# Graph layer with GNN, linear attention and expert FFN: 127-partition loads in two pieces, sample tables earlier, one more staged chunk in the sort stage, FFN block gathers moved into the GNN loop

## The chip, the core and the metric

One core of one Trainium2 chip runs the kernel. The metric is the device time of one execution in microseconds. Times inside the run are those of one profiled execution. The engines are called TensorE (PE in rows; PEld is its weight load), VectorE (DVE), ScalarE (ACT), GpSimd (POOL) and SyncE (SP); a row with SPq, ACTq or POOLq is the issue of a DMA by that engine.

## What is computed

There are 6250 nodes with 256 features, x. The reference, cut to what matters:

```python
xn = layernorm(x)
x = x + gnn(xn, src, dst) + mix(xn)        # gnn: 100000 edges sorted by dst
x = x + ffn(layernorm(x))                  # ffn: 131072 edges, not sorted
# gnn, per head: e = leaky(e_src[src] + e_dst[dst])
#   out[n] = sum over edges with dst = n of softmax(e) * z[src]
# mix: linear attention; k = softmax over nodes, context = k^T v, q softmax over dims
# ffn: graph attention gives scores per expert; top 2 of 4 experts, GELU FFN each
```

Edges of one graph lie sorted by dst, 784 (GNN) or 1024 (FFN) on each of 128 partitions, 100000 = 127 * 784 + 432. The softmax and sum over the edges of a node is then a scan along each partition.

## The kernel before

The program is a row of blocks, each a list of instructions per engine that runs in order; an all-engine barrier ends each block. Order inside an engine is the order written; between engines there are semaphores only. Three blocks are touched.

**Sort and projection** (`project`, L645). VectorE sorts the FFN edges by dst with a bitonic network (`dve_stages`); between pieces of it, `sort_on(n)`, it makes layernorm statistics of x (`stats`, `norm`, in 7 groups of 7 tiles). TensorE turns and projects each tile into rows z (L816), ScalarE copies them out, SyncE stores them in HBM (`gnn_rows`). Then TensorE makes keys and values (L410), and ScalarE stores v rows in HBM.

In the same block the place where each node's edges begin is found (`search_parts`, L241): dst comes in (L714: 127 partitions; the tail of 432 on partition 127 through GpSimd, L764), VectorE copies it to `edges` and takes every 28th as `few` (L926 to L929, `dst_ready`). SyncE writes `few` and `edges` to HBM (L717, L718) and reads `few` back twice, the second time one row lower, `table[0:127]` into `above[1:128]` (L272 to L274). VectorE compares all nodes with row starts (`dve_first`, L281) and splits the differences of samples (`dve_rise`, L287 to L300); TensorE multiplies both (`pe_samples`, L309); VectorE counts and gives a block number per node (`dve_blocks`, L315 to L325). GpSimd then gathers one block of 28 dst per node, 50 indirect DMAs (`pool_blocks`, L331), VectorE counts in it (`dve_base`, `dve_places`, L337 to L367), and GpSimd scatters row starts (`scatter_starts`, L965, 50 DMAs). Before them GpSimd has issued the loads of Wqkv (L766) and src (L768, L770), with x's groups coming through ScalarE's queue (0 and 1) and SyncE's (2 before `dst_ready`, 3 to 6 after the samples).

When z is stored, GpSimd gathers z rows by src, one indirect DMA per column of 128 edges. The GNN loop later goes over 56 chunks of 14 columns with 4 buffers (`got`). Six chunks, `STAGED`, don't go straight into a buffer: GpSimd gathers them ahead in halves of 7 columns into `staged` (`pool_half`, L450), SyncE writes each half to HBM (`sp_half`, L457), and in the loop one large load brings a chunk back (`sp_staged`, L1417). `STAGED_WITH_SORT` of the six are done in this block, and behind them the first two chunks are gathered into their buffers (`first_gathers`, L1215).

**Keys** (`key_context`, L1072). GpSimd gathers the other staged halves, then chunks 2 and 3. VectorE takes the maximum of k over nodes (L1172), subtracts it (L1190), and does the search for the FFN graph as above up to block numbers (L277 to L325), then spreads row starts over edges (`dve_all`, L1013 to L1054) and scales the context (L1200). ScalarE takes exp. TensorE sums k^T v (L1146) over 13 loads of v with two buffers; after the sixth load's sums stand the sample products of the search (L309), and at the end two small turns for `dve_all`. SyncE's list: search samples, row starts, v loads 0 and 1, three staged halves, then alternately one v load and one of the remaining halves. A v load from the third on waits for the sums two loads before.

**GNN loop** (`gnn_edges`, L1583). Per chunk c VectorE makes logits (L1296 to L1317), weighs the gathered rows (L1367) and scans (L1391); ScalarE takes exp, weighs one head (L1378), writes states out (L1407); TensorE and the others do one tile of the attention output beside. GpSimd gathers chunk c from 4 on into buffer c modulo 4 (`pool_gather`, L1277, 14 DMAs) once chunk c - 4 is weighed, unless c is staged. After the loop it gathers the 50 blocks of the FFN search (`pool_blocks`, L331). SyncE stores states and tiles and ends by waiting for them. The next block (`carry`) begins with a barrier and uses the gathered blocks.

Of the kernel before, what the change touches and what calls it, by code (L numbers as in the profile page):

```python
# [16 lines left out]
P = 128  # L17
# [9 lines left out]
NS = NT + 1  # L27

# [9 lines left out]
STAGED = (8, 14, 21, 28, 36, 44)  # L38
STAGED_WITH_SORT = 4
# [80 lines left out]
class Kernel:  # L120
# [120 lines left out]
    def search_parts(self, g, stack):  # L241
# [22 lines left out]
        class Steps:  # L264
# [5 lines left out]
            def sp_samples(sp):  # L270
# [3 lines left out]
                sp.dma_start(above[1:P, :], table[0:P - 1, :]).then_inc(samples_in, 16)  # L274
# [9 lines left out]
            def dve_rise(dve):  # L284

                dve.wait_ge(samples_in, 32)
# [358 lines left out]
    def project(self, kv, kv_done, parts, later, staging):  # L645
# [7 lines left out]
        with ExitStack() as here:  # L653
# [25 lines left out]
                     "dst_tail_in", "src_tail_in", "wqkv_in",  # L679
                     "stats_made", "root_made", "norm_ready", "xn_ready", "turned", "xt_ready", "projected", "z_evac", "xt_out", "starts_out", "minus_set")  # L680
            (padded, dst_in, dst_ready, samples_out, blocks_out, w_in, att_clear, w_turned, w_ready, zeroed, seg_clear, src_in,
             dst_tail_in, src_tail_in, wqkv_in,
# [28 lines left out]
            def _(sp):  # L711
                sort.sp_load(sp)
                sp.wait_ge(padded, 1)
                sp.dma_start(dst_i[0:full, :], io["dst"][0:full * GNN.width].rearrange("(p w) -> p w", w=GNN.width)).then_inc(dst_in, 16)  # L714
                load_x(sp, 2)
# [5 lines left out]
                for g in range(3, LOADS):  # L721
                    load_x(sp, g)
# [30 lines left out]
                sp.wait_ge(src_tail_in, 16)  # L753
                sp.wait_ge(wqkv_in, 16)
# [5 lines left out]
            def _(pool):  # L760
# [4 lines left out]
                               io["dst"][full * GNN.width:GNN.edges].rearrange("(p w) -> p w", p=1)).then_inc(dst_tail_in, 16)  # L765
                pool.dma_start(self.wqkv[:, :, :], io["L0_mix_Wqkv"].rearrange("(k p) c -> p k c", p=P)).then_inc(wqkv_in, 16)  # L766
# [3 lines left out]
                pool.dma_start(self.edge_src["gnn"][0:full, 0:GNN.width],  # L770
                               io["src"][0:full * GNN.width].rearrange("(p w) -> p w", w=GNN.width)).then_inc(src_in, 16)
# [8 lines left out]
                pool.wait_ge(src_tail_in, 16)  # L780
                for j in range(2 * STAGED_WITH_SORT):
                    staging.pool_half(pool, j)
# [110 lines left out]
            def _(dve):  # L893
# [30 lines left out]
                dve.wait_ge(dst_in, 16)  # L924
# [5 lines left out]
                dve.drain()  # L930
                stats(0)
# [3 lines left out]
                find.dve_first(dve, later)  # L935
                find.dve_rise(dve)
# [135 lines left out]
    def key_context(self, kv, kv_done, stack, find, context, later, parts, staging):  # L1072
# [6 lines left out]
        with ExitStack() as mine:  # L1079
# [23 lines left out]
            def _(sp):  # L1103
# [12 lines left out]
                halves = iter(range(2 * STAGED_WITH_SORT, 2 * len(STAGED)))  # L1116
                for j in (next(halves), next(halves), next(halves)):
                    staging.sp_half(sp, j)
                for g in range(SLOTS, loads):
                    load_v(g)  # L1120
                    for j in halves:
                        staging.sp_half(sp, j)
                        break
# [459 lines left out]
    def gnn_edges(self, fin, finm, parts, ctx, find):  # L1583
# [7 lines left out]
        with ExitStack() as here:  # L1591
# [41 lines left out]
            def _(pool):  # L1633
                def step(c, b, u, i):
# [1091 lines left out]
```

## Time and profile before

| | us |
|---|---|
| median of 3 runs | 2831.59 (2829.88 to 2832.51) |
| the profiled execution | 2831.12 |
| its span, first to last instruction | 2829.3 |
| sort and projection | 0 to 336.9 |
| keys | 336.9 to 438.9 |
| GNN loop | 438.9 to 1354.5 |
| all that follows | 1354.5 to 2829.3 |

The span is what the trace covers, 1.8 us less than the execution's time. Busy over the span: VectorE 74%, GpSimd 69%, TensorE 53%, ScalarE 46%. These shares are means over stages with different limits, so a stage has to be read by itself: by who comes last to its barrier, and what that engine waited for. An idle time in brackets behind an instruction is the time its engine stood before it, and the arrow names what ended it; "issue" is time in which it waited for nothing that the profile shows.

### The profile page before, as it was taken

How to read it: one execution, taken by the hardware profiler on the slowest of the kernel's cores; microseconds unless marked ns; L12 is line 12 of the kernel's file. 1: busy time of each engine (PE TensorE's matmuls, PEld its weight loads, DVE VectorE, ACT ScalarE, POOL GpSimd, SP SyncE). 2: the span in 40 equal slices, each digit the busy share in tenths (PEclk: the TensorE clock that was granted, in tenths of full speed). 3: DMA queues.
4: the chain of work that ended last, by engine and by line, in shares of the span. 5: the costliest groups of instructions: out<-in, count | busy, mean ns of one | idle time of the engine just before them, and what ended most of it. 6: DMA issues, size and time to landing. Idle time of an engine off the chain costs nothing. (4 is left out here: it accounts for less than half of the span.)

```text
span 2829.3 us, 22764 instructions
## 1 busy us (share of the span) xinstructions
PE 1511.8 (53%) x5476; PEld 938.2 (33%) x5476; DVE 2083.0 (74%) x3305; ACT 1302.0 (46%) x3173; POOL 1943.4 (69%) x1982
## 2 busy tenths in 40 slices
PE   2766440123232323331152399999999999984223
PEld 2533140011111111110052266555555555551023
DVE  6988769899999999995493566556555555567557
ACT  2622116799999999995152122222222222220022
POOL 1677675767777777777466877777777777777560
PEclk9978775555555555555555699999999999997666
DMA  5717664777777877774651322222222222222195
GB/s 160 238 28 207 200 207 143 261 243 257 252 252 259 274 237 274 242 244 140 190 163 48 100 51 51 54 53 62 52 53 51 51 50 51 50 57 40 34 317 220
DMA packets 225713, 418.38 MB, mean 148 GB/s; under 512 B 51232, under 2 KB 174733, under 8 KB 218156
## 3 DMA queue, kind: packets, MB, share of 16 engines
q1 hardware_dynamic: 133504, 278.19, 27.8%
q0 software_dynamic: 75920, 123.77, 19.6%
q10 hardware_dynamic: 16156, 14.98, 1.6%
q8 instruction: 44, 0.72, 0.1%
q14 instruction: 89, 0.73, 0.1%
HBM read 216.03 MB, written 200.77 MB: 147 GB/s over the span
## 5 line engine op out<-in xcount | busy, mean ns | idle before, releaser
L1277 POOL DMA_INDIRECT stage_got<-ffn_rows,setup_src_ffn x860 | 839.3, 976 | 261.9 <-issue 261.8
L1277 POOL DMA_INDIRECT edges_got<-gnn_rows,edges_src_gnn x644 | 610.0, 947 | 246.7 <-issue 192.2
L1391 DVE TENSOR_TENSOR_SCAN stage_y<-stage_decays,stage_y 128x960 f32<-128x960 f32 (+2 forms) x256 | 520.7, 2088 | 5.8 <-issue 5.7
L2221 PE MATMUL stage_ph<-ffn_xt_all,stage_w 128*128 128x448 f32 x896 | 372.5, 555 | 98.7 <-ACT stage_start_parts L2282 39.6
L1407 ACT ACTIVATE stage_rows<-stage_y 128x3640 f32<-128x3640 f32 (+1 forms) x88 | 400.7, 4553 | 0.0
L2343 DVE TENSOR_TENSOR stage_start_parts<-stage_pk,stage_of_tile 128x490 f32<-128x490 f32 x328 | 209.4, 666 | 115.2 <-PE stage_pk L2213 110.9
L2213 PE MATMUL stage_pk<-stage_start_parts 128*128 128x490 bf16 x984 | 252.4, 396 | 65.5 <-DVE stage_start_parts L2343 51.0
L1693 PE MATMUL stage_pm<-setup_ident,stage_mix_parts 128*128 128x128 f32 x98 | 32.4, 434 | 432.6 <-ACT stage_mix_parts L1716 423.3
L1367 DVE TENSOR_TENSOR stage_y<-edges_got,stage_weights 128x896 f32<-128x896 f32 x168 | 262.6, 1665 | 0.3 <-ACT stage_weights L1346 0.3
L2221 PEld LDWEIGHTS stage_ph<-ffn_xt_all,stage_w 128*128 128x128 f32 x896 | 170.0, 192 | 236.5 <-issue 137.9
L2346 DVE TENSOR_REDUCE stage_got<-stage_start_parts 128x20 f32<-128x980 f32 x164 | 192.6, 1174 | 15.6 <-issue 0.9
L1349 ACT ACTIVATE stage_y<-stage_chunk_parts 128x128 f32<-128x128 f32 x32 | 9.9, 311 | 416.5 <-DVE stage_chunk_parts L1317 416.5
L2361 DVE TENSOR_TENSOR search_found<-stage_po,stage_b 128x512 f32<-128x512 f32 x112 | 70.0, 625 | 178.1 <-PE stage_po L2233 171.7
L1378 ACT ACTIVATE stage_y<-edges_got,stage_y 128x64 f32<-128x64 f32 x784 | 197.4, 422 | 0.0
L2233 PE MATMUL stage_po<-stage_w,stage_hid 128*128 128x256 f32 x784 | 183.9, 380 | 0.0
L2233 PE MATMUL stage_po<-stage_w,stage_start_parts 128*128 128x256 f32 x784 | 183.0, 380 | 0.0
L1693 PEld LDWEIGHTS stage_pm<-setup_ident,stage_mix_parts 128*128 128x128 f32 x98 | 14.2, 203 | 466.5 <-DVE stage_mix_parts L1766 453.4
L2213 PEld LDWEIGHTS stage_pk<-stage_start_parts 128*128 128x128 bf16 x984 | 93.8, 102 | 216.3 <-DVE stage_start_parts L2343 94.2
L2233 PEld LDWEIGHTS stage_po<-stage_w,stage_hid 128*128 128x128 f32 x784 | 150.7, 192 | 39.1 <-issue 18.2
L2233 PEld LDWEIGHTS stage_po<-stage_w,stage_start_parts 128*128 128x128 f32 x784 | 149.3, 190 | 36.5 <-issue 14.8
L1681 PE MATMUL stage_pq<-stage_mix_parts 128*128 128x256 f32 x196 | 100.1, 665 | 84.2 <-ACT stage_mix_parts L1730 84.2
L2282 ACT ACTIVATE stage_start_parts<-stage_ph,stage_b 128x896 f32<-128x896 f32 x56 | 55.1, 1007 | 192.1 <-PE stage_ph L2221 192.0
(483 smaller groups left out, 3099.5 us busy)
## 6 DMA issues: line engine op xcount, KB each, us to landing
state_gnn<-stage_rows SPq DMA_DIRECT2D x56, 1848.0 KB, 7.4
y<-search_found SPq DMA_DIRECT2D x28, 896.0 KB, 4.2
tail_fin_y<-y SPq DMA_DIRECT2D x7, 3584.0 KB, 17.1
stage_got<-ffn_rows,setup_src_ffn POOLq DMA_INDIRECT x860
state_ffn<-stage_rows SPq DMA_DIRECT2D x32, 384.0 KB, 2.4
edges_got<-gnn_rows,edges_src_gnn POOLq DMA_INDIRECT x700, 3.8
staged_rows<-rows_staged SPq DMA_DIRECT2D x12, 910.0 KB, 4.7
edges_got<-staged_rows SPq DMA_DIRECT2D x6, 1820.0 KB, 13.9
```

The lines of the kernel that those rows point to most:

```text
L1277: pool.indirect_dma_start(out=got[:, u, t, :], out_offset=None, in_=self.row_dram[g.name][:, :], in_offset=bass.IndirectOffsetOnAxis(ap=sr ...
L1367: ins = dve.tensor_tensor(of_head(h, s)[:, :, :, 0:n].rearrange("p q k t -> p t q k"), mine.rearrange("p t (q k) -> p t q k", q=Q), weight ...
L1378: ins = act.activation(of_head(h, s)[:, :, :, t], got[:, u, t, h * K:(h + 1) * K].rearrange("p (q k) -> p q k", q=Q), ACT.Copy, scale=y[:, ...
L1391: ins = dve.tensor_tensor_scan(some, r[s][:, 0:b - a, :].rearrange("p c t -> p (c t)"), some, 0.0, ALU.mult, ALU.add)
L1407: act.activation(rows[:, s, :, 0:C + H], y[:, s, :, 1:T + 1].rearrange("p c t -> p t c"), ACT.Copy).then_inc(rows_ready, 1)
L1681: mm = pe.matmul(pq[:, 0:D], xt[:, slot, k * P:(k + 1) * P], wq[:, k, :], start=(k == 0), stop=(k == 1))
L2213: mm = pe.matmul(pk[:, a, 0:(r1 - r0) * NT], chosen[:, c % 2, j * P:(j + 1) * P], table[:, n, r0:r1, :].rearrange("p r t -> p (r t)"), sta ...
L2221: mm = pe.matmul(ph[:, f % 2 * 2 + half, 0:HALF], w1[:, e, k, f * P:(f + 1) * P], xt_all[:, k, at(b * (B * P) + half * HALF, HALF)], start ...
L2233: mm = pe.matmul(po[:, bank, side:side + D], hid[s][:, f, t * P:(t + 1) * P], w2[:, e, f, :], start=(f == 0), stop=(f == FT - 1))
L2343: dve.tensor_tensor(masked[:, r0:r1, :], pk[:, a, 0:(r1 - r0) * NT].rearrange("p (r t) -> p r t", t=NT), of_tile[:, j, :].unsqueeze(1).to_ ...
L2346: dve.tensor_reduce(got[:, c % 2, T - picked(FFN, c) + j, :], masked, AX, ALU.add)
L2361: dve.tensor_tensor(yrow[:, k * 2:k * 2 + n, :], po[:, k % 2, 0:n * D].rearrange("p (t d) -> p t d", d=D), b2[:, e, :].unsqueeze(1).to_bro ...
```

## The change

Loads of 127 partitions are issued as 112 (`EVEN`) and 15: dst, src, and the read-back of the samples one row lower, in both searches. In the sort block, x's group 2 and Wqkv are issued after `dst_ready`, and `dve_first` and `dve_rise` come ahead of the statistics of group 0. Five staged chunks instead of four are gathered in the sort block; in the keys block SyncE writes the two halves left one after the other, ahead of the third v load. In the GNN loop GpSimd gathers 18 of the FFN blocks before chunk 4, five at each staged chunk, and two at the end.

```diff
+EVEN = P - 16
-STAGED_WITH_SORT = 4
+STAGED_WITH_SORT = 5
+BLOCKS_FIRST, BLOCKS_EACH = 18, 5
...
@@ sp_samples (L270), dve_rise (L284)
-                sp.dma_start(above[1:P, :], table[0:P - 1, :]).then_inc(samples_in, 16)
+                sp.dma_start(above[1:EVEN + 1, :], table[0:EVEN, :]).then_inc(samples_in, 16)
+                sp.dma_start(above[EVEN + 1:P, :], table[EVEN:P - 1, :]).then_inc(samples_in, 16)
...
-                dve.wait_ge(samples_in, 32)
+                dve.wait_ge(samples_in, 48)
...
@@ project, sync (L711)
-                sp.dma_start(dst_i[0:full, :], io["dst"][0:full * GNN.width].rearrange("(p w) -> p w", w=GNN.width)).then_inc(dst_in, 16)
-                load_x(sp, 2)
+                for a, b in ((0, EVEN), (EVEN, full)):
+                    sp.dma_start(dst_i[a:b, :], io["dst"][a * GNN.width:b * GNN.width].rearrange("(p w) -> p w", w=GNN.width)).then_inc(dst_in, 16)
...
-                for g in range(3, LOADS):
+                for g in range(2, LOADS):
                     load_x(sp, g)
...
@@ project, gpsimd (L760)
+                pool.wait_ge(dst_ready, 1)
                 pool.dma_start(self.wqkv[:, :, :], io["L0_mix_Wqkv"].rearrange("(k p) c -> p k c", p=P)).then_inc(wqkv_in, 16)
...
-                pool.dma_start(self.edge_src["gnn"][0:full, 0:GNN.width],
-                               io["src"][0:full * GNN.width].rearrange("(p w) -> p w", w=GNN.width)).then_inc(src_in, 16)
+                pool.dma_start(self.edge_src["gnn"][0:EVEN, 0:GNN.width],
+                               io["src"][0:EVEN * GNN.width].rearrange("(p w) -> p w", w=GNN.width)).then_inc(src_in, 16)
+                pool.dma_start(self.edge_src["gnn"][EVEN:full, 0:GNN.width],
+                               io["src"][EVEN * GNN.width:full * GNN.width].rearrange("(p w) -> p w", w=GNN.width)).then_inc(src_rest_in, 16)
...
@@ project, vector (L893)
-                dve.wait_ge(dst_in, 16)
+                dve.wait_ge(dst_in, 32)
...
+                find.dve_first(dve, later)
+                find.dve_rise(dve)
                 stats(0)
                 sort_on(1)
                 norm(0)
                 stats(1)
-                find.dve_first(dve, later)
-                find.dve_rise(dve)
                 norm(1)
...
@@ key_context, sync (L1103)
-                halves = iter(range(2 * STAGED_WITH_SORT, 2 * len(STAGED)))
-                for j in (next(halves), next(halves), next(halves)):
+                for j in range(2 * STAGED_WITH_SORT, 2 * len(STAGED)):
                     staging.sp_half(sp, j)
                 for g in range(SLOTS, loads):
                     load_v(g)
-                    for j in halves:
-                        staging.sp_half(sp, j)
-                        break
...
@@ gnn_edges, gpsimd (L1633)
+                few = self.search_few(FFN)
+
                 def step(c, b, u, i):
-                    if c >= GNN.slots and c not in STAGED:
+                    if c == GNN.slots:
+                        find.pool_blocks(pool, few, range(BLOCKS_FIRST))
+                    if c in STAGED:
+                        done = BLOCKS_FIRST + STAGED.index(c) * BLOCKS_EACH
+                        find.pool_blocks(pool, few, range(done, done + BLOCKS_EACH))
+                    elif c >= GNN.slots:
                         edge.pool_gather(pool, c, b, u)
                 in_quads(step)
-                find.pool_blocks(pool, self.search_few(FFN), range(NS))
+                find.pool_blocks(pool, few, range(BLOCKS_FIRST + len(STAGED) * BLOCKS_EACH, NS))
```

## Rows read from the trace of the kernel before

**Rows 1.** Busy time by stage: start:end, length, busy us (instructions) of each engine, TensorE clock, DMA share, GB/s.
```profile
0.00:336.90 336.90, 190.60 (x718) 109.71 (x718) 267.29 (x588) 111.59 (x336) 201.78 (x203) 0.85 0.53 160
336.90:438.90 102.00, 36.37 (x307) 33.62 (x307) 72.65 (x76) 13.12 (x8) 68.12 (x58) 0.68 0.62 194
438.90:1354.50 915.60, 236.56 (x496) 130.70 (x496) 847.63 (x987) 808.56 (x2116) 659.87 (x694) 0.50 0.71 238
```

**Rows 2.** VectorE in order of time, stage one: start, us, instruction [idle before <- what ended it].
```profile
35.21 0.57 DVE L926 CAST project_sorted_dst<-project_dst_i 128x784 f32<-128x784 int32 x1 [14.84 <-DMA project_dst_i<-in_dst_dram]
45.03 6.83 DVE L281 TENSOR_TENSOR edges_later_nodes<-setup_lane,project_search_gnn 128x6400 bf16<-128x6400 f32 x1
336.91 0.09 DVE L268 MEMSET earch_search_ffn_samples<- 1x32 f32 x1 [13.56 <-PEq L162]
```

**Rows 3.** Two stretches of stage one, columns as in the first group.
```profile
4.50:19.50 15.00, 0.00 (x0) 0.00 (x0) 8.57 (x34) 1.28 (x1) 2.97 (x5) 1.00 0.97 291
26.00:34.50 8.50, 2.25 (x12) 2.15 (x10) 0.00 (x0) 2.08 (x5) 0.00 (x0) 1.00 0.07 26
```

**Rows 4.** GpSimd in order of time, stage one.
```profile
61.42 1.08 POOL L331 DMA_INDIRECT search_found<-blocks_gnn,ject_search_gnn_at_block  x1 [53.94 <-DVE ject_search_gnn_at_block L325]
143.21 1.20 POOL L965 DMA_INDIRECT seg_gnn<-setup_start_rows_gnn,setup_seg_at_gnn  x1 [13.29 <-DVE setup_end_at_gnn L367]
327.90 0.95 POOL L1215 DMA_INDIRECT edges_got<-gnn_rows,edges_src_gnn  x1 [0.30 <-issue]
```

**Rows 5.** VectorE in order of time, stage two.
```profile
408.36 0.17 DVE L315 TENSOR_SCALAR search_search_ffn<-keys_tp 128x15 f32<-128x15 f32 x1 [23.50 <-PE keys_spread L309]
```

**Rows 6.** TensorE in order of time, stage two.
```profile
366.35 5.64 PE L1146 MATMUL keys_pkv<-keys_v_in,rows_X 128*128 128x129 f32 x32 [4.44 <-ACT rows_X L1162]
377.09 3.62 PE L1146 MATMUL keys_pkv<-keys_v_in,rows_X 128*128 128x129 f32 x16 [5.11 <-DMA keys_v_in<-v_rows]
394.58 5.20 PE L1146 MATMUL keys_pkv<-keys_v_in,rows_X 128*128 128x129 f32 x32 [13.87 <-DMA keys_v_in<-v_rows]
405.35 1.90 PE L309 MATMUL keys_tp<-ch_search_ffn_rise_parts,edges_later_nodes 128*128 128x33 bf16 x60
```

**Rows 7.** SyncE in order of time, stage two: issues, merged where alike.
```profile
370.21 0.37 SPq L1112 DMA_DIRECT2D keys_v_in<-v_rows  x1
387.30 0.32 SPq L457 DMA_DIRECT2D staged_rows<-rows_staged  x1
```

**Rows 8.** VectorE, the last chunk of the GNN loop.
```profile
1290.60 0.24 DVE L1296 TENSOR_TENSOR stage_chunk_parts<-edges_got,edges_ed_edge 128x56 f32<-128x56 f32 x1
```

**Rows 9.** Groups of GpSimd in stage three: count | busy us, mean ns | idle before, what ended it.
```profile
L1277 POOL DMA_INDIRECT edges_got<-gnn_rows,edges_src_gnn x644 | 610.0, 947 | 246.7 <-issue 192.2 <-DVE stage_y L1367 28.9 <-ACT stage_y L1378 25.6
L331 POOL DMA_INDIRECT search_found<-blocks_ffn,arch_search_ffn_at_block x50 | 49.8, 997 | 15.2 <-issue 15.2
```

**Rows 10.** GpSimd in order of time, first and last gather of stage three.
```profile
447.14 0.94 POOL L1277 DMA_INDIRECT edges_got<-gnn_rows,edges_src_gnn  x1 [24.05 <-ACT stage_y L1378]
1278.90 0.95 POOL L1277 DMA_INDIRECT edges_got<-gnn_rows,edges_src_gnn  x1 [0.30 <-issue]
```

**Rows 11.** Waits of SyncE around the end of stage three: us in total, times, longest.
```profile
SPq L1591 <- PEq L1591: 24.8, 1, 24.8
```

**Rows 12.** DMA issues: count, KB each, median us from issue to landing.
```profile
project_keys<-in_L_ffn_edge_index_dram SPq DMA_DIRECT2D x2, 512.0 KB, 5.5
samples_gnn<-project_few_dst SPq DMA_DIRECT2D x1, 14.0 KB, 2.4
keys_v_in<-v_rows SPq DMA_DIRECT2D x12, 516.0 KB, 5.7
edges_got<-gnn_rows,edges_src_gnn POOLq DMA_INDIRECT x700, 3.8
```

**Rows 13.** Groups of GpSimd, 130 to 336 us: the staged gathers of stage one.
```profile
L450 POOL DMA_INDIRECT rows_staged<-gnn_rows,edges_src_gnn x56 | 59.1, 1056 | 19.6 <-issue 16.5 <-DMA staged_rows<-rows_staged 1.7 <-DMA seg_gnn<-setup_start_rows_gnn,setup_seg_at_gnn 1.4
```

**Rows 14.** GpSimd, one staged gather of stage two.
```profile
367.53 1.63 POOL L450 DMA_INDIRECT rows_staged<-gnn_rows,edges_src_gnn  x1 [0.30 <-issue]
```

More of the change, by code:

```diff
@@ L678, in project @@
             names = ("padded", "dst_in", "dst_ready", "samples_out", "blocks_out", "w_in", "att_clear", "w_turned", "w_ready", "zeroed", "seg_clear", "src_in",
-                     "dst_tail_in", "src_tail_in", "wqkv_in",
+                     "dst_tail_in", "src_tail_in", "src_rest_in", "wqkv_in",
                      "stats_made", "root_made", "norm_ready", "xn_ready", "turned", "xt_ready", "projected", "z_evac", "xt_out", "starts_out", "minus_set")
             (padded, dst_in, dst_ready, samples_out, blocks_out, w_in, att_clear, w_turned, w_ready, zeroed, seg_clear, src_in,
-             dst_tail_in, src_tail_in, wqkv_in,
+             dst_tail_in, src_tail_in, src_rest_in, wqkv_in,
              stats_made, root_made, norm_ready, xn_ready, turned, xt_ready, projected, z_evac, xt_out, starts_out, minus_set) = (self.sem(here, n) for n in names)
@@ L753, in _ @@
                 sp.wait_ge(src_tail_in, 16)
+                sp.wait_ge(src_rest_in, 16)
                 sp.wait_ge(wqkv_in, 16)
@@ L780, in _ @@
                 pool.wait_ge(src_tail_in, 16)
+                pool.wait_ge(src_rest_in, 16)
                 for j in range(2 * STAGED_WITH_SORT):
```

## The prediction

> **What bounds the kernel now.** I read the span by stage first [rows 1]. The change touches the first three stages only (to 1354.5 us); the 1474.8 us behind them keep their code. A stage ends at a barrier, so in each one I ask which engine arrives last; the chain of waits covers only the end of the run and says nothing here.
>
> Stage one (sort and projection, to 336.9): VectorE stands 14.84 us before its copy of dst, and is done 13.56 us before the barrier opens [rows 2]. Meanwhile, the 26 to 34.5 us stretch has DMA at 0.07 of 16 engines and 26 GB/s [rows 3]: one engine carries the load's tail. The queue that is last is GpSimd's: its first block gather waits for VectorE until 61.42, its first scatter until 143.21, then it runs without pause to 328.9 (327.90 + 0.95), some 8 us ahead of the barrier [rows 4]. So GpSimd ends this stage, and VectorE moves GpSimd only through those two waits.
>
> Stage two (keys, to 438.9) ends with VectorE, which loses 23.50 us there, waiting for TensorE's sample products [rows 5]. TensorE has them behind six loads of v, and its longest pauses are for loads three and four [rows 6]. SyncE issues loads in the order written: after load three (370.21) it stands until 387.30 for a staged half that GpSimd has not gathered, and only then issues load four [rows 7].
>
> Stage three (GNN loop, to 1354.5): VectorE's last chunk starts at 1290.60 [rows 8]; after its last gather (1278.90) GpSimd issues 50 block gathers, 65.0 us, and the stage ends at 1354.5 [rows 9, 10]. SyncE, with all else stored, waits 24.8 us at this barrier [rows 11]. That overhang is what the third edit is aimed at.
>
> **The change, part by part.** The profiled execution took 2831.12 us, its span is 2829.3; the median of the three runs is 2831.59, 0.47 above. I sum against 2831.1.
>
> *dst as 112 + 15.* 388.9 KB at 26 GB/s is 15 us [rows 3], the length of the wait. What the split load takes isn't in this trace. Above: it lands no sooner (35.2). Below: one engine's 26 GB/s times 16 would be 1 us. The nearest row is the keys' 512 KB, 128 partitions on the same queue, 5.5 us from issue to landing [rows 12]; behind them, dst should land at about 13 to 16 us. VectorE needs it at 20.4 (35.21 less 14.84), so the whole wait of 14.84 goes; 5 us of slack stay.
> The Trainium skill's page "DMA: Bandwidth & Descriptors", section "Why a DMA increments its semaphore by 16 and not by 1", says a copy goes to the largest number of engines up to 16 that divides its outer dimension: 127 rows to 1, 112 to 16, 15 to 15. By that rule the load would be near the 1 us end, and the sum would be the same; the 0.07 share agrees with it for 127.
>
> *Samples first.* dst is ready at 21.3 instead of 36.1. The samples go out (2.4 us [rows 12]) and come back by three DMAs instead of two, one more issue of 0.3 us on SyncE: landed by about 27. VectorE covers this with its compare at L281, 6.83 us [rows 2], now ahead of stats(0), to 28.6. If the cover fails, the late side is a load like keys', 5.5 us, 2 us late: 0 taken, 2 kept for the range. x's third load and later ones are issued after the samples, and the 768 KB of Wqkv wait on GpSimd for dst; 5.4 MB at the 291 GB/s of the first busy stretch [rows 3] end at about 43 us; VectorE needs the third group, 1.7 MB with Wqkv beside it and so there at about 31, at 38, and the fourth past 50. GpSimd's src loads are behind Wqkv now and needed only by the staged gathers past 195: 0. Their split adds one issue on GpSimd, before the wait for VectorE: 0. Splitting the second search's samples adds one SyncE issue, before loads that nobody waits for yet: 0.
>
> *Stage one's end.* Both of GpSimd's waits come 15 us earlier. Then ten staged halves instead of eight: 14 more gathers at (59.1 + 19.6)/56 = 1.40 us [rows 13], 19.7 us. VectorE ends its sort 15 us earlier, and gathers that run after it cost 1.25 (rate of stage three, (610.0 + 192.2)/644 [rows 9]) instead of 1.35: some 18 of them, 2 us. GpSimd ends at 328.9 - 15 + 19.7 - 2 = 331.6. **Stage one: +2 us** (bounds -2 and +6); what VectorE gains is only waited longer at the barrier.
>
> *Stage two.* GpSimd has two staged halves left, done 18 us into the stage; SyncE stores both and then holds the v loads for TensorE's sums alone. In the old time base: loads one and two are summed from 366.35 on, 2.8 us each [rows 6]; load three is issued at 369.3 and lands, with the 5.7 us of its row [rows 12], at 375; three and four are summed to 381.2 (3.6 and 2.6 us), five issued at 378.6 and six at 381.2, six is summed by 389.5, and the samples take 3.0 (405.35 to 408.36): 392.5 against 408.36, 15.9 us earlier. With 6.9 us per load, as 370.21 to 377.09 shows, it is 13.5; with 4 it is 19. Behind the samples TensorE still has seven loads, as before, so the rest moves with it; 1 us off for pauses. **Stage two: -15 us** (bounds -20 and -9).
>
> *Stage three.* 48 of 50 block gathers go into the loop, ahead of GNN gathers: 18 first, five at each staged chunk. One is (49.8 + 15.2)/50 = 1.30 us [rows 9], the 48 are 62.4 us. GpSimd had idle time in the loop: 8.2 us at its start (438.9 to 447.14 [rows 10]), some 30 later, 8 at the end; less than 62. So GpSimd becomes the bound, and its queue is a floor: 644 gathers at 1.25 are 805, and 438.9 + 805 + 62.4 = 1306.3. The last rows land 2.9 later (3.8 from issue [rows 12], less 0.95): chunk 55 starts at 1309.2 instead of 1290.60, 18.6 us late. Bounds: 17.5 if the landing is quick, 24 with 1.40 per block gather. What follows chunk 55 is unchanged, and two block gathers lie beside it. The barrier opens 24.8 earlier for the overhang and 18.6 later for the loop. **Stage three: -6 us** (bounds -7 and 0).
>
> Sum: +2 - 15 - 6 = -19; 2831.1 - 19 = **2812 us**, 0.7% under the median.
>
> **The rivals.**
> 1. *The loop hides the block gathers.* VectorE was the loop's bound and GpSimd waited 28.9 + 25.6 us in it [rows 9]. Then chunk 55 keeps its time and stage three gives all 24.8: 2831.1 + 2 - 15 - 24.8 = 2793. Against: 24.05 of that idle is one wait, of which only 8.2 us lie in this stage. Chance 0.07.
> 2. *TensorE's wait is the v loads themselves.* If their latency, and not SyncE's order, sets loads four to six, stage two gives nothing: 2827. For: loads five to six also paused it. Against: the 17 us between two issues on SyncE. Chance 0.08.
> 3. *dst is no faster*, or the time goes to x and the keys' loads in front of it, so the split doesn't do what it says: GpSimd keeps its 61.42 and stage one is +17 instead of +2: 2827. Chance 0.06.
> 4. *Slower: VectorE holds up the inserted gathers.* In stage two, beside VectorE's large subtracts, a staged gather took 1.63 us instead of 0.95 [rows 14], 0.68 more. At that price 48 gathers add 33 us to a queue that is the bound: 2812 + 33 = 2845. It decides from 0.4 us each on (19/48). Against: the loop's gathers have a mean of 947 ns beside VectorE's scans and products [rows 9], no more than the quick ones anywhere. The Trainium skill's page "SBUF — State Buffer", section "Who interferes with whom", has VectorE and GpSimd share one port pair, which an instruction holds to its end. By that rule alone 2845 would be the time to expect wherever VectorE's instructions take the pair; the mean in the loop shows that they mostly don't there. Chance 0.06.
> 5. *Stages one and two give more* (quicker v loads, gathers at 1.25 throughout): 2803. Chance 0.08.
>
> **How the numbers follow.** The forecast has 0.65, with a range of its own from 2804 to 2821. Rivals 1 to 5 have 0.07, 0.08, 0.06, 0.06, 0.08. The range 2800 to 2828 takes in cases 2, 3 and 5 and leaves out 1 and 4 and some tails. A measurement tells 0.2% from no change here, 5.7 us: faster is below 2825.9. Rivals 2 and 3 fall within 0.2%, rival 4 is slower; faster 0.82, same 0.11, slower 0.07.
>
> **What would show it.** Stage one right: no wait of VectorE for dst, GpSimd's first block gather near 46, its last gather near 331, the stage's end near 339, with VectorE waiting over 25 us at the barrier. Stage two right: VectorE's 23.50 falls to 5 to 10, the loads of v follow each other without SyncE's gap, the stage takes 87 instead of 102. Stage three right: GpSimd without waits of any length, chunk 55's logits waiting for gathered rows, a loop 18 us longer and no overhang. It is wrong if GpSimd still waits for VectorE late in the loop (rival 1), if inserted gathers are longer than 1.1 us (rival 4), or if VectorE's dst wait stays (rival 3).

## The result, and the profile after

The changed kernel takes 2814.47 us (median of 4 runs, 2813.73 to 2815.70) against 2832.05 for the kernel before (4 runs on the same chip): a ratio of 0.9933, 95% interval 0.9919 to 0.9946, 17.6 us less. The profiled execution has a span of 2812.5 us, 16.8 under the 2829.3 of before. The windows by stage (start:end, length, busy us of PE, PEld, DVE, ACT, POOL, granted TensorE clock, DMA share, GB/s) answer to [rows 1]:

```profile
0.00:342.00 342.00, 192.25 (x718) 110.84 (x718) 267.45 (x588) 111.35 (x336) 217.28 (x217) 0.83 0.56 169
342.00:423.50 81.50, 33.19 (x306) 30.42 (x307) 72.71 (x76) 13.16 (x8) 54.62 (x44) 0.73 0.62 196
423.50:1334.40 910.90, 236.85 (x496) 130.69 (x496) 849.00 (x987) 807.15 (x2116) 660.52 (x695) 0.50 0.71 239
1334.40:2812.50 1478.10, 1046.33 (x3956) 663.36 (x3956) 896.98 (x1654) 368.25 (x714) 1017.30 (x1028) 0.84 0.34 86
```

| stage | before | after | difference | forecast |
|---|---|---|---|---|
| sort and projection | 336.9 | 342.0 | +5.1 | +2 |
| keys | 102.0 | 81.5 | -20.5 | -15 |
| GNN loop | 915.6 | 910.9 | -4.7 | -6 |
| the rest | 1474.8 | 1478.1 | +3.3 | 0 |
| span | 2829.3 | 2812.5 | -16.8 | -19 |

**Stage one.** VectorE in order of time (start, us, instruction, in brackets the idle time before it and what ended it), answering to [rows 2]:

```profile
19.99 0.57 DVE L934 CAST project_sorted_dst<-project_dst_i 128x784 f32<-128x784 int32 x1
...
21.78 6.83 DVE L284 TENSOR_TENSOR edges_later_nodes<-setup_lane,project_search_gnn 128x6400 bf16<-128x6400 f32 x1
31.27 0.19 DVE L290 TENSOR_TENSOR oject_search_gnn_samples<-oject_search_gnn_samples 128x28 f32<-128x28 f32 x1 [2.66 <-DMA oject_search_gnn_samples<-samples_gnn]
...
342.06 0.09 DVE L270 MEMSET earch_search_ffn_samples<- 1x32 f32 x1 [30.93 <-PEq L164]
```

The wait for dst is gone: the copy starts at 19.99 and nothing stands before it. In its place stands a wait of 2.66 us for the samples at L290, behind the compare that was to cover them. SyncE's issues show the samples on their way in time, and GpSimd's show what was issued beside them, and the waits that answer to [rows 4]:

```profile
23.51 1.11 SPq L276 DMA_DIRECT2D oject_search_gnn_samples<-samples_gnn  x1
24.67 0.44 SPq L277 DMA_DIRECT2D oject_search_gnn_samples<-samples_gnn  x1
```

```profile
21.20 0.79 POOL L771 DMA_DIRECT2D edges_got<-in_L_mix_Wqkv_dram  x1 [15.57 <-DVE project_few_dst L937]
...
49.26 1.07 POOL L334 DMA_INDIRECT search_found<-blocks_gnn,ject_search_gnn_at_block  x1 [25.69 <-DVE ject_search_gnn_at_block L328]
...
129.59 1.22 POOL L973 DMA_INDIRECT seg_gnn<-setup_start_rows_gnn,setup_seg_at_gnn  x1 [11.65 <-DVE setup_end_at_gnn L370]
...
331.91 0.95 POOL L1219 DMA_INDIRECT edges_got<-gnn_rows,edges_src_gnn  x1 [0.30 <-issue]
342.01 0.78 POOL L1011 IOTA keys_start_parts<- 128x784 int32 x1 [9.15 <-POOLq L164]
```

The samples' last read-back is issued at 24.67 and is there only at 31.27. In the microseconds ahead of it GpSimd issued Wqkv (768 KB, at 21.20) and src, and SyncE the 392 KB of block keys (at 21.32). In the five profiles with this order the wait is 1.41 to 2.66 us. GpSimd's first block gather moves from 61.42 to 49.26, 12.2 us where I had 15; from there to its last gather (331.91) it has one pause of length, the scatter's 11.65. What VectorE gained it waits for at the barrier, 30.93 us instead of 13.56.

**Stage two.** VectorE's 23.50 of [rows 5] is 2.89:

```profile
392.92 0.18 DVE L318 TENSOR_SCALAR search_search_ffn<-keys_tp 128x15 f32<-128x15 f32 x1 [2.89 <-PE keys_spread L312]
```

TensorE (where [rows 6] showed pauses of 5.11 and 13.87) and SyncE (where [rows 7] showed 17 us between two issues):

```profile
371.51 5.98 PE L1150 MATMUL keys_pkv<-keys_v_in,rows_X 128*128 128x129 f32 x32 [4.44 <-ACT rows_X L1166]
379.19 2.05 PE L1150 MATMUL keys_pkv<-keys_v_in,rows_X 128*128 128x129 f32 x16 [1.71 <-DMA keys_v_in<-v_rows]
...
385.10 2.05 PE L1150 MATMUL keys_pkv<-keys_v_in,rows_X 128*128 128x129 f32 x16 [1.38 <-DMA keys_v_in<-v_rows]
...
390.17 1.68 PE L312 MATMUL keys_tp<-ch_search_ffn_rise_parts,edges_later_nodes 128*128 128x33 bf16 x60 [0.65 <-DVE ch_search_ffn_rise_parts L303]
```

```profile
356.25 6.93 SPq L460 DMA_DIRECT2D staged_rows<-rows_staged  x2
375.37 0.37 SPq L1120 DMA_DIRECT2D keys_v_in<-v_rows  x1
```

SyncE issues the eleven later loads without a staged half between them. TensorE's pauses for the next four loads are 1.71, 0.42, 1.38 and 0.32 us, and the sample products start at 390.17 because VectorE's own operands (L303) come only then. The sums of one load take 2.05 us, where [rows 6] has 3.62 and half of 5.20. The windows of those sums, columns as in the windows by stage, first two of before, then one of after, differ in TensorE's granted clock: 0.55 and 0.73 of full speed, means of the two levels of 1.2 and 2.4 GHz, behind pauses of 5.11 and 13.87 us, against 1.00, the upper level throughout, behind one of 1.71:

```profile
377.05:380.75 3.70, 3.62 (x16) 3.43 (x16) 3.70 (x1) 0.76 (x1) 3.54 (x1) 0.55 0.14 37
394.58:399.80 5.22, 5.20 (x32) 5.01 (x32) 0.00 (x0) 0.00 (x0) 4.00 (x5) 0.73 0.80 232
379.19:389.55 10.36, 8.21 (x64) 7.44 (x64) 9.96 (x13) 3.40 (x2) 9.51 (x3) 1.00 0.68 209
```

From issue to landing a load of v takes 4.2 us, not the 5.7 of [rows 12] (count, KB each, median us):

```profile
keys_v_in<-v_rows SPq DMA_DIRECT2D x12, 516.0 KB, 4.2
```

Over the profiles with the new order it is 4.1 to 4.6 us; with the old order it is 5.7, and 4.9 in two others, so part of the 5.7 was that one profile's.

**Stage three.** GpSimd's groups (count, busy us, mean ns, idle before and what ended it) answer to [rows 9], then VectorE's logits, before and after:

```profile
L1281 POOL DMA_INDIRECT edges_got<-gnn_rows,edges_src_gnn x644 | 610.5, 948 | 196.2 <-issue 194.9 <-ACT stage_y L1382 0.9 <-DVE stage_y L1371 0.3
L334 POOL DMA_INDIRECT search_found<-blocks_ffn,arch_search_ffn_at_block x50 | 50.0, 1001 | 29.9 <-POOLq L164 14.9 <-issue 14.9
```

```profile
L1296 DVE TENSOR_TENSOR stage_chunk_parts<-edges_got,edges_ed_edge 128x56 f32<-128x56 f32 x56 | 13.3, 238 | 0.1
L1300 DVE TENSOR_TENSOR stage_chunk_parts<-edges_got,edges_ed_edge 128x56 f32<-128x56 f32 x56 | 13.3, 238 | 22.1 <-DMA edges_got<-gnn_rows,edges_src_gnn 22.0
```

GpSimd's waits for VectorE and ScalarE in the loop, 28.9 and 25.6 us before, are 0.3 and 0.9: its queue is full. VectorE, which had 0.1 us of idle time in front of these logits before, waits 22.0 us for gathered rows. In order of time, VectorE's first instruction behind the barrier before; then VectorE and GpSimd after, where [rows 8] and [rows 10] stood:

```profile
1354.65 0.28 DVE L1522 MEMSET carry_gnn_mend_parts<- 128x264 f32 x1 [32.11 <-PEq L162]
```

```profile
1294.99 0.26 DVE L1300 TENSOR_TENSOR stage_chunk_parts<-edges_got,edges_ed_edge 128x56 f32<-128x56 f32 x1 [1.61 <-DMA edges_got<-gnn_rows,edges_src_gnn]
...
1334.51 0.28 DVE L1526 MEMSET carry_gnn_mend_parts<- 128x264 f32 x1 [7.59 <-PEq L164]
```

```profile
447.65 0.96 POOL L1281 DMA_INDIRECT edges_got<-gnn_rows,edges_src_gnn  x1 [0.30 <-issue]
...
1294.79 1.01 POOL L334 DMA_INDIRECT search_found<-blocks_ffn,arch_search_ffn_at_block  x1 [0.30 <-issue]
1334.39 0.31 POOL L1466 MEMSET carry_gnn_carry_parts<- 4x260 f32 x1 [38.59 <-POOLq L164]
```

Chunk 55 starts 871.5 us after the stage began (before: 851.7). Behind its last block gather GpSimd stands 38.59 us, and VectorE waits 7.59 for the barrier instead of 32.1. The overhang is gone, and nearly all of it was paid for in the loop.

### The profile page after: what moved, and what is told of

Its sections match the earlier page's. It is cut to its first block and busy times, and to the rows that moved or that the text cites. A ratio compares the mean times of both kernels' runs of the same rounds, so it can differ in the third digit from the quotient of the medians.

```text
span 2812.5 us, 22777 instructions
## 1 busy us (share of the span) xinstructions
PE 1508.6 (54%) x5476; PEld 935.3 (33%) x5476; DVE 2086.1 (74%) x3305; ACT 1299.9 (46%) x3173; POOL 1949.7 (69%) x1983
```

## The experiments

Twelve runs, one kernel twice among them. Ratios are to the kernel before on the same chip, with 95% intervals; the stages are those of each run's profile.

| run | time, us | ratio | stage one | keys | loop | rest |
|---|---|---|---|---|---|---|
| changed kernel | 2814.5 | 0.9933 | 342.0 | 81.5 | 910.9 | 1478.1 |
| blocks at the end | 2818.5 | 0.9956 (0.9939 to 0.9972) | 342.0 | 81.5 | 916.0 | 1479.7 |
| 24 blocks in the loop | 2794.2 | 0.9870 (0.9853 to 0.9886) | 341.3 | 81.4 | 891.4 | 1479.9 |
| dst whole | 2823.5 | 0.9973 (0.9963 to 0.9982) | 350.9 | 81.5 | 911.1 | 1481.5 |
| split alone | 2820.0 | 0.9955 (0.9938 to 0.9971) | 322.3 | 99.9 | 916.6 | 1478.6 |
| weights late | 2812.0 | 0.9932 (0.9915 to 0.9948) | 338.4 | 81.4 | 910.8 | 1481.1 |
| four with the sort | 2812.5 | 0.9926 (0.9910 to 0.9943) | 322.4 | 95.8 | 912.8 | 1479.5 |
| 24 blocks, weights late | 2793.8 | 0.9861 (0.9844 to 0.9877) | 339.4 | 81.4 | 891.7 | 1480.3 |
| three edits | 2792.8 | 0.9850 (0.9833 to 0.9866) | 320.8 | 97.3 | 891.3 | 1479.6 |
| three edits, again | 2787.5 | 0.9844 (0.9830 to 0.9857) | 321.2 | 96.0 | 891.5 | 1475.9 |
| first search part early | 2794.9 | 0.9859 (0.9842 to 0.9875) | 323.0 | 95.8 | 891.5 | 1482.6 |
| both search parts early | 2782.3 | 0.9818 (0.9804 to 0.9831) | 315.4 | 96.2 | 891.6 | 1486.2 |
| before, a second profile | 2835.5 | one run | 335.6 | 102.1 | 916.4 | 1479.6 |

**Is GpSimd's queue the floor of the loop? All 50 block gathers at the end again.**

```diff
-        if c == GNN.slots:
-            find.pool_blocks(pool, few, range(BLOCKS_FIRST))
-        if c in STAGED:
-            done = BLOCKS_FIRST + STAGED.index(c) * BLOCKS_EACH
-            find.pool_blocks(pool, few, range(done, done + BLOCKS_EACH))
-        elif c >= GNN.slots:
+        if c >= GNN.slots and c not in STAGED:
             edge.pool_gather(pool, c, b, u)
     in_quads(step)
-    find.pool_blocks(pool, few, range(BLOCKS_FIRST + len(STAGED) * BLOCKS_EACH, NS))
+    find.pool_blocks(pool, few, range(NS))
```

> The changed kernel with its third edit undone: all 50 FFN block gathers go behind GpSimd's last GNN gather again. Theory (in the changed kernel GpSimd's queue is the floor of the GNN loop, and in the old one its 50 gathers hang over the loop's end): chunk 55 starts 851 to 853 us after the loop's stage begins instead of 871.5, VectorE's 12 waits for gathered rows (22 us) go, the overhang comes back, and the stage takes 915 to 917 us instead of 910.9; the kernel 2818 to 2820, 4 to 5 us over the changed one. Rival (the loop is 20 us longer for another reason, such as the contention that the earlier stages' new layout brings): chunk 55 stays near 871, and the stage takes 930 or more, the kernel about 2835. The 1478 us after the loop are untouched: if the 3.3 us that they gained belong to the third edit, they are 1475 here, if to the run, anything between 1474 and 1479.

The loop's stage takes 916.0 us and chunk 55 starts 851.6 us into it. GpSimd's waits for the two others come back, and VectorE's for rows fall to nothing:

```profile
L1281 POOL DMA_INDIRECT edges_got<-gnn_rows,edges_src_gnn x644 | 610.7, 948 | 244.3 <-issue 190.2 <-DVE stage_y L1371 28.1 <-ACT stage_y L1382 26.0
```

So the 20 us in the loop are the 48 gathers and nothing else of the change. The edit as it was made is worth 5 us of the loop's stage, and 4 us of the time.

**A smaller share in the loop.**

```diff
-BLOCKS_FIRST, BLOCKS_EACH = 18, 5
+BLOCKS_FIRST, BLOCKS_EACH = 6, 3
```

> The changed kernel with 24 block gathers in the loop instead of 48 (6 first, 3 at each staged chunk, 26 at the end). Theory (GpSimd's floor against VectorE's own time): 24 gathers at 1.30 us are 31 us, so the floor puts chunk 55 at 805 + 31 + 3 = 839 us after the stage's start, below VectorE's own 852; VectorE becomes the bound, chunk 55 starts at 852 to 856, and the 26 gathers at the end (34 us from 840, and 8 to 9 us to drain) end before VectorE's 39 us behind chunk 55: the stage takes 891 to 896 us, the kernel 2795 to 2800. Rival one (block gathers cost VectorE or the rows' landing time by themselves, about 0.4 us each): 20 us for 48 become 10 for 24, chunk 55 at 862, the stage 901, the kernel 2805. Rival two (the drain of the gathers at the end is longer than thought, so the overhang returns): chunk 55 at 852 but the stage above 900.

GpSimd's and VectorE's groups in the loop:

```profile
L1281 POOL DMA_INDIRECT edges_got<-gnn_rows,edges_src_gnn x644 | 611.0, 949 | 201.6 <-issue 190.8 <-DVE stage_y L1371 6.2 <-ACT stage_y L1382 4.6
```

```profile
L1300 DVE TENSOR_TENSOR stage_chunk_parts<-edges_got,edges_ed_edge 128x56 f32<-128x56 f32 x56 | 13.3, 238 | 0.1
```

891.4 us, at the low end of what the theory said: VectorE waits 0.1 us for rows, so it sets the pace again (GpSimd waits 10.8 for it and ScalarE), and the 26 gathers behind the loop end beside VectorE's tail of 39 us. The drain is no issue, nor are the block gathers by themselves. The third edit is right in direction and moved too many: 0 in the loop give 916, 48 give 911, 24 give 891. Other counts weren't tried.

**Was it the one engine? dst in one piece again.**

```diff
-for a, b in ((0, EVEN), (EVEN, full)):
+for a, b in ((0, full),):
-dve.wait_ge(dst_in, 32)
+dve.wait_ge(dst_in, 16)
```

> The changed kernel with dst loaded by one DMA of 127 partitions again, all else kept. Theory (the one-engine load was the wait): VectorE's copy of dst waits 12 to 16 us again and starts at 32 to 36; the load shows 25 to 30 GB/s; the first block gather moves from 49.3 to 58 to 62, the wait for the samples stays between 0 and 3; stage one ends 8 to 15 us later (350 to 357), since GpSimd's queue is full behind it; the kernel 2823 to 2829. Rival (the loads in front of dst, not its one engine, made the wait, and the order of the loads has cured it): the wait is under 4 us and the kernel within 3 us of the changed one.

```profile
30.32 0.57 DVE L934 CAST project_sorted_dst<-project_dst_i 128x784 f32<-128x784 int32 x1 [10.07 <-DMA project_dst_i<-in_dst_dram]
...
40.34 0.19 DVE L290 TENSOR_TENSOR oject_search_gnn_samples<-oject_search_gnn_samples 128x28 f32<-128x28 f32 x1 [1.41 <-DMA oject_search_gnn_samples<-samples_gnn]
```

The wait is back, and stage one is 8.9 us longer; but it is 10.07 us, less than the 12 I had as its least. From 20 to 30 us the DMA line of the trace reads:

```profile
DMA packets 120, 0.25 MB, mean 25 GB/s; under 512 B 3, under 2 KB 59, under 8 KB 120
...
q1 hardware_dynamic: 62, 0.19, 4.8%
q10 hardware_dynamic: 58, 0.06, 1.6%
```

25 GB/s in all, and the two queues that move something have 4.8 and 1.6% of sixteen engines' time, together 6.4%, or one engine of sixteen: SyncE's with dst and ScalarE's with the end of a load of x. By the Trainium skill's page "DMA: Bandwidth & Descriptors", section "Why a DMA increments its semaphore by 16 and not by 1", 127 rows go to one engine; that share agrees. The other 4.8 us of the old 14.84 went with the order: Wqkv, src and x's third load, now behind `dst_ready`, no longer stand beside this load. Which of the three it was wasn't tried.

**The split and nothing else, on the kernel before.**

```diff
+for a, b in ((0, EVEN), (EVEN, full)):
+    sp.dma_start(dst_i[a:b, :], ...)
-sp.dma_start(dst_i[0:full, :], ...)
-dve.wait_ge(dst_in, 16)
+dve.wait_ge(dst_in, 32)
```

> The kernel before with dst loaded as 112 and 15 partitions, and nothing else changed. Theory (the split removes the wait, and GpSimd's queue carries the gain to the barrier, as there are still eight staged halves beside the sort): VectorE's wait for dst falls from 14.84 to under 1 us, the first block gather comes at 46 to 48 instead of 61.4, stage one ends at 322 to 324 instead of 336.9; stages two (102) and three (916) stay; the kernel 2816 to 2818. Rival (as the whole load without Wqkv and the third load of x beside it took 10 us of waiting instead of 14.8, these cost dst 4.8 us, and cost it as much when it is split): the wait stays at 4 to 5 us, stage one ends at 327, and the kernel is 2821.

```profile
20.41 0.57 DVE L928 CAST project_sorted_dst<-project_dst_i 128x784 f32<-128x784 int32 x1
...
46.64 1.08 POOL L332 DMA_INDIRECT search_found<-blocks_gnn,ject_search_gnn_at_block  x1 [39.15 <-DVE ject_search_gnn_at_block L326]
...
391.73 0.17 DVE L316 TENSOR_SCALAR search_search_ffn<-keys_tp 128x15 f32<-128x15 f32 x1 [21.40 <-PE keys_spread L310]
```

With Wqkv beside it the split load is still there before VectorE asks (no wait at 20.41), so the rival falls, and stage one ends at 322.3. The keys keep a wait of 21.40. This one edit gives 12.4 us, where the whole change gives 17.6. The time, 2820.0, is 2 us over what was expected; the three stages are within 1 us of it or shorter, and the rest is longer (1478.6 against 1474.8).

The first block gather comes at 46.64, 2.6 us before the changed kernel's 49.26. Taking the compare and the samples ahead of the statistics brought GpSimd's first wait nothing: VectorE has the same work in front of the block numbers in either order, and the new order added the wait for the samples. With four staged chunks stage one ends at 322.3 here and at 322.4 with the new order ("four with the sort"); where that wait is taken away as well ("three edits") it ends at 320.8 and 321.2, a gain no larger than the 1.3 us between the two profiles of the kernel before (336.9 and 335.6). So in stage one the runs show a gain for the split, and none beyond that spread for the order.

**The wait for the samples.**

```diff
-pool.wait_ge(dst_ready, 1)
+pool.wait_ge(samples_in, 48)
 pool.dma_start(self.wqkv[:, :, :], ...)
```

> The changed kernel with GpSimd's loads of Wqkv and src (1.16 MB) held until the samples are back, instead of until dst is ready. Theory (VectorE's new wait of 2.66 us for the samples is their DMA sharing the engines with Wqkv and src, issued in the same microseconds): the wait falls under 0.5 us, the first block gather comes at 46 to 47 instead of 49.3, stage one ends 2 to 3 us earlier, the kernel 2811 to 2812.5. Rival one (the 392 KB of block keys, on the samples' own queue ahead of their read-back, or the third DMA's 1.1 us of issue, make the wait): it stays at 2 us or more and the time at 2814. Rival two (Wqkv comes too late then): TensorE's projection waits for it, the scatter's wait grows, and the kernel is 2815 or slower.

```profile
21.86 6.82 DVE L284 TENSOR_TENSOR edges_later_nodes<-setup_lane,project_search_gnn 128x6400 bf16<-128x6400 f32 x1
28.61 0.18 DVE L293 TENSOR_TENSOR oject_search_gnn_samples<-oject_search_gnn_samples 128x28 f32<-128x28 f32 x1
```

```profile
25.98 0.79 POOL L774 DMA_DIRECT2D edges_got<-in_L_mix_Wqkv_dram  x1 [20.35 <-DMA oject_search_gnn_samples<-samples_gnn]
...
46.58 1.07 POOL L337 DMA_INDIRECT search_found<-blocks_gnn,ject_search_gnn_at_block  x1 [18.23 <-DVE ject_search_gnn_at_block L331]
```

With Wqkv and src issued at 25.98, the samples are there when VectorE's compare ends: the wait is gone, the first block gather is 2.7 us earlier and stage one ends 3.6 earlier (with the 24 blocks 1.9: 339.4 against 341.3). So those two loads made the wait; the block keys, still ahead of the samples on their queue, didn't by themselves, and the issue at L276, 1.11 us in the changed kernel, is 0.43 us here. The kernel's time, 2812.0, can't be told from the changed one's by itself; the rows can.

**What held the loads of v: SyncE's order or the number of halves?** Four staged chunks beside the sort, so again four halves in the keys' stage; the last two are gathered behind chunks 2 and 3 and stored behind the last load of v.

```diff
-STAGED_WITH_SORT = 5
+STAGED_WITH_SORT = 4
 # GpSimd
+halves = range(2 * STAGED_WITH_SORT, 2 * len(STAGED))
-for j in range(2 * STAGED_WITH_SORT, 2 * len(STAGED)):
+for j in halves[0:2]:
     staging.pool_half(pool, j)
 ...
+for j in halves[2:]:
+    staging.pool_half(pool, j)
 # SyncE
-for j in range(2 * STAGED_WITH_SORT, 2 * len(STAGED)):
+for j in halves[0:2]:
     staging.sp_half(sp, j)
 for g in range(SLOTS, loads):
     load_v(g)
+for j in halves[2:]:
+    staging.sp_half(sp, j)
```

> The changed kernel with four staged chunks beside the sort instead of five, so that the keys' stage again has four staged halves as the kernel before; but only two of them stand between the loads of v, and the other two are gathered behind GpSimd's first gathers and stored behind all loads of v. Theory (SyncE's order held the loads of v, the number of halves in the stage did not; and GpSimd ends stage one): VectorE's wait for the sample products stays at 2 to 5 us instead of going back to 23.5; stage one loses 14 gathers, 18 to 19 us, and ends at 323 to 325, with VectorE's wait at its barrier falling from 31 to 12; in the keys' stage GpSimd works 19 us longer, to about 86 us after its start, 9 more to drain, so the stage takes 94 to 97 us instead of 81.6; the sum is 5 us less and the kernel 2808 to 2811. Rival (the halves themselves, by their traffic or by GpSimd, kept the loads of v late): VectorE's wait is over 10 us, VectorE ends the stage at over 100 us, and the kernel is 2818 or more.

```profile
373.29 0.18 DVE L318 TENSOR_SCALAR search_search_ffn<-keys_tp 128x15 f32<-128x15 f32 x1 [2.89 <-PE keys_spread L312]
```

```profile
410.29 0.95 POOL L453 DMA_INDIRECT rows_staged<-gnn_rows,edges_src_gnn  x1 [0.30 <-issue]
418.90 1.02 POOL L334 DMA_INDIRECT search_found<-blocks_ffn,arch_search_ffn_at_block  x1 [7.66 <-POOLq L164]
```

SyncE's waits for the gathers of staged halves in the keys' stage of the kernel before (us in total, times, longest):

```profile
SPq L457 <- DMA rows_staged<-gnn_rows,edges_src_gnn: 45.6, 4, 16.7
```

VectorE's wait is 2.89 again with twice the halves, so the order was the cause. SyncE waits for them here as it did before (42.6 us, 16.6 the longest), but the long wait, which stood between loads three and four of v, now stands behind the last of them. SyncE's order alone, on the kernel before, wasn't run. Stage one loses 19.6 us and the keys gain 14.3: GpSimd ends them now (its last gather at 410.29, the barrier 7 us later). The time came out 1.5 us above the range I gave; the loop had 1.9 us more.

**The 1478 us behind the loop.** The kernel before, unchanged.

> The kernel before, unchanged, for a second profile of it. Open is where the 3.3 us of the 1478 us behind the loop come from, which no edit touches. If they are the run's, this profile has 1477 to 1481 us behind the loop, as the profiles of the changed kernels have (1478.0 to 1481.5); if they come with the change (its code's place, or its buffers'), it has 1474 to 1476 again. Stages one to three: 337, 102 and 916.

1479.6: the rest is not 3.3 us longer for the change. Over the fourteen profiles of this untouched code it runs from 1474.8, the first profile of before, to 1486.2.

**Together.** The diffs are those above: first 24 blocks and the late weights, then four staged chunks with them.

> The changed kernel with 24 instead of 48 block gathers in the loop, and Wqkv and src held until the samples are back: the two runs that gained, together. Theory (they act in different stages, one by the loop's floor and one by the queue of stage one): the gains add, stage one ends at 338 to 339, stage three takes 891 to 892, and the kernel is 2790 to 2793. Rival (with less work of GpSimd's in front of it, something of stage one comes back in the loop, or the 2.5 us were the run's): 2794 to 2796.

> The changed kernel with three edits together: 24 block gathers in the loop instead of 48, Wqkv and src held until the samples are back, four staged chunks beside the sort with the last two staged halves behind the loads of v. Theory (three stages, three bounds, so the gains add): stage one ends at 319 to 321, the keys' stage takes 95 to 97 us, the loop's stage 891 to 893, the kernel 2787 to 2790. Rival (the staged halves that end later, or 14 more gathers at the end of the keys' stage, delay the loop's start): the loop's stage takes 895 or more, the kernel 2793 or more.

The stages come as expected (339.4 and 891.7; then 320.8, 97.3 and 891.3). The times don't follow to the microsecond: the first (2793.8) is 0.8 us above its range; the second is above its range on one chip (2792.8) and in it on another (2787.5, under what I had for that second run), with the ratio to before nearly the same (0.9850 and 0.9844).

**GpSimd's start in stage one.** On the three edits, first `dve_blocks` earlier, then `dve_base` and what follows too.

```diff
 stats(0)
+find.dve_blocks(dve, banks, found_few)
 sort_on(1)
 ...
 stats(2)
-find.dve_blocks(dve, banks, found_few)
```

> The same, and the block search's VectorE part of stage one directly behind stats(0), ahead of a sort step, two norms and two stats. Theory (GpSimd's queue is full from its first block gather to the barrier, so what it starts earlier it ends earlier): the first block gather comes 8 to 9 us earlier, at 38 to 39; stage one follows until VectorE's own end binds: VectorE stores its keys at 310 and their DMA has to land, so it ends at 313 to 315 instead of 320, and VectorE's wait at the barrier shrinks to 3 to 5 us; the kernel 2781 to 2785. Rival (GpSimd waits longer for its scatter instead, since VectorE's second search step keeps its place behind the sort): the wait of 11.6 us before the scatter grows to about 20, stage one ends at 319 to 321 as without this edit, the kernel as the other.

```profile
38.02 1.26 POOL L337 DMA_INDIRECT search_found<-blocks_gnn,ject_search_gnn_at_block  x1 [9.63 <-DVE ject_search_gnn_at_block L331]
...
129.69 1.22 POOL L976 DMA_INDIRECT seg_gnn<-setup_start_rows_gnn,setup_seg_at_gnn  x1 [23.63 <-DVE setup_end_at_gnn L373]
```

The rival: 8.7 us earlier at the first block gather, all of it given back at the scatter (23.63 us of waiting instead of 11.7), as VectorE's second part stayed where it was. Stage one did not gain (323.0 against 320.8), nor did the time (2794.9 against 2792.8 on the same chip).

```diff
-sort_on(15)
+sort_on(7)
 find.dve_base(dve, found_few)
```

> The last kernel with the block search's second VectorE part also earlier: 7 sort steps instead of 15 ahead of it (the other 8 behind it, at 1.37 us each 11 us). Theory (in the last run GpSimd's 8.7 us came back as a longer wait before its scatter, 23.63 us, because VectorE's second part stayed at 120.3): the second part starts at 109 to 110, the scatter at 118 to 120 instead of 129.7, and stage one ends at 312 to 315, where VectorE's stored keys bind; VectorE's wait at the barrier falls from 12.3 to 2 to 5 us; the keys' stage and the loop's stay at 96 and 891; span 2780 to 2784, time 2782 to 2787. Rival (the rows of GNN nodes, which TensorE, ScalarE and SyncE make, hold the staged gathers then): the first staged gather waits over 5 us for them, and stage one ends at 318 or later, the kernel at 2789 or more.

> The kernel with the three edits once more, on the same chip as the one above, so that the two are compared without a change of chip: 2789 to 2794, stages as in its first run (320.8, 97.3, 891.3); theory: 5 to 8 us over the one above; rival: the same time.

```profile
119.44 1.22 POOL L976 DMA_INDIRECT seg_gnn<-setup_start_rows_gnn,setup_seg_at_gnn  x1 [12.68 <-DVE setup_end_at_gnn L373]
...
315.43 0.78 POOL L1014 IOTA keys_start_parts<- 128x784 int32 x1 [11.16 <-POOLq L164]
```

```profile
315.48 0.09 DVE L270 MEMSET earch_search_ffn_samples<- 1x32 f32 x1 [4.10 <-PEq L164]
```

With both parts moved the scatter starts at 119.44 and stage one ends at 315.4, just past the range: GpSimd is idle for 11.16 us before the barrier instead of 8.0, and VectorE waits 4.10, so here the bound passes from GpSimd's queue to VectorE's sort and the store of its keys, which SyncE issues from 311.40 on, when VectorE has them, and then waits for. This version beats both kernels: 0.9818 of before, against 0.9933 for the change, and 5 us under the three edits on the same chip (2787.5). Its profile caught the slowest of five executions (span 2789.4), with 1486.2 us behind the loop.

## Why the prediction was right, and where it was off

The forecast of 2812 is 2.5 us below the median of 2814.5. In each stage the mechanism was the one forecast; the sizes were off by +3.1, -5.5 and +1.3 us. That these nearly cancel is luck; the rest added its 3.3.

- *Stage one, +2, measured +5.1.* The mechanism held: GpSimd's queue ends the stage, the split removed the wait, a fifth staged chunk was put on. The failed step is "0 taken, 2 kept" for the samples: 2.66 us. I priced their way by a quiet write of 2.4 us [rows 12] and looked at what Wqkv would do to x, not to the samples. Without that wait the stage is +1.5 (338.4) or +2.5 (339.4 in the run with 24 blocks). "Samples first" as such had no gain in the sum, and shows none. GpSimd was done at 332.9 for 331.6, and the barrier came 9.15 us behind it where before it was 8.02.
- *Stage two, -15, measured -20.5.* SyncE's order was the cause, as said. Mis-sized are two terms of the working. A load of v, 5.7 us there, takes 4.2; why it is shorter isn't shown (with four halves and 28 gathers in the stage it is 4.4). The sums of a load, 3.6 and 2.6 us there, take 2.05, at a granted clock of 1.00; the working took them as fixed. Done again, it gives 19 us for the quicker load alone and about 21 for both (estimates, before the 1 us for pauses). VectorE's wait fell by 20.6. The measured value is half a microsecond past the end of the range.
- *Stage three, -6, measured -4.7.* Chunk 55 was to start 870.3 us into the stage and started at 871.5; the barrier for the overhang came 24.5 earlier, for 24.8. The floor (count of gathers times 1.25 or 1.30) is the best-sized term here.
- *The rest, 0.* Right: 3.3 us are within what one profile differs from the next, as the second profile of before (1479.6) shows.

The rivals: the loop didn't hide the block gathers (first); TensorE's wait was not the loads' own latency (second, by the run with four halves); dst did get faster (third). The fifth is half right: stage two gave more, stage one less. The fourth, the slower one, didn't come: the block gathers, 48 of 50 of them now beside VectorE in the loop, had a mean of 1001 ns, against 997 at the end before. The Trainium skill's page "SBUF — State Buffer", section "Who interferes with whom", would have an instruction of VectorE's that holds the port pair hold them up; the trace doesn't show it in this loop. In the keys' stage it does: the gather that the changed kernel issues at 382.37 lasts 6.94 us, beside VectorE's compare of 6.82 us at 381.67.

## What to carry to other kernels

Work moved from behind a loop into it is hidden only up to the idle time of the queue that issues it: count the queue as instructions times interval, put that much inside, and leave as much behind as another engine's tail covers. A duration read from one stretch of one profile is not a constant: the loads of v and the sums on them were both shorter once nothing stood between them. A small transfer that an engine waits for can pay for bulk loads issued just ahead of it, here with up to 2.66 us. Work put earlier in an engine's order gains nothing where the same work still stands in front of what is waited for. An earlier start pays only as far as the next thing that the queue waits for: move the whole chain or none of it.

## What was not expected of the hardware

The load on one engine took about 5 us longer with other loads beside it (14.84 us of waiting against 10.07), while the split load, with the same loads beside it, was not waited for. And code that no edit touches takes 1474.8 to 1486.2 us from one profile to the next, 0.4% of the span: more than several of these edits are worth, so that they show in a stage's rows before they show in the time. Open is why the barrier of stage one comes 9.15 us after GpSimd goes idle with five staged chunks beside the sort and 8.0 with four.
